# Four moves of work inside the blocks of a Mamba-style mixer with an MLP behind it: token copy, padded x, fold of squares, last half projection

## The reference, cut to what matters

```
x = x + mixer(layernorm(x))          # the part that the change touches
x = x + ffn(layernorm(x))            # silu(gate) * up, then down, inner width 1408

mixer:
  proj = x @ W_in * mup              # z (1024), xBC (1024+128+128), dt (64)
  xBC  = silu(causal conv of 4 taps) # gives x, B, C
  dt   = softplus(dt + bias);  dA = exp(-dt * exp(A_log))
  state = state * dA + (dt * x) outer B ;  y = state . C      # per token, 64 heads of 16
  g    = (y + D * x) * silu(z)
  g    = g * rsqrt(mean(g^2) + eps) * norm_w
  out  = g @ W_out
```

## Time and profile before

| what | value |
|---|---|
| median of the timed runs | 776.65 us |
| the profiled execution | 781.25 us |
| its span, first to last instruction | 779.5 us |
| mean granted TensorE clock | 0.987 |
| TensorE busy | 742.5 us, 95% of the span |
| VectorE, ScalarE, GpSimd busy | 66%, 63%, 38% |

### The profile page before, as it was taken

How to read it: one execution, slowest core, us unless ns; L and a number is a source line. 1 busy time by engine, 2 the same in 40 slices (tenths; PEclk the granted TensorE clock), 3 DMA queues, 4 the chain that set the end, 5 groups by cost and what they waited for, 6 DMA issues and landing times.

```text
span 779.5 us, 20312 instructions
## 1 busy us (share of the span) xinstructions
PE 742.5 (95%) x8486; PEld 611.1 (78%) x8486; DVE 517.5 (66%) x845; ACT 492.0 (63%) x933; POOL 294.5 (38%) x235
## 2 busy tenths in 40 slices
PE   4977999999999999999999999889999999999998
PEld 4855788788887887887878888668888888888887
DVE  6968976986887797797787698773633532632431
ACT  5989878978978977978878797633322321331330
POOL 3163275366456536627708628530011011001002
PEclk9988999999999999999999999999999999999999
DMA  9823244484475266355355367754113004002002
GB/s 304 228 62 109 45 102 112 96 235 130 82 215 163 79 146 209 101 148 187 109 160 185 108 182 241 227 168 155 62 49 114 0 28 132 3 3 94 11 1 84
DMA packets 42299, 94.97 MB, mean 122 GB/s; under 512 B 9888, under 2 KB 15776, under 8 KB 42016
## 3 DMA queue, kind: packets, MB, share of 16 engines
q1 hardware_dynamic: 42208, 93.67, 41.8%
HBM read 84.73 MB, written 17.57 MB: 131 GB/s over the span
## 4 chain that ended last, share of the span: by engine, by line
PE 72%; DVE 16%; ACT 6%; issue 3%; DMA 2%; SPq 1%; POOL 0%; DVEq 0%; ACTq 0%; POOLq 0%
PE ps_y L1678 10%; PE ps_proj L1665 9%; DVE cx L936 7%; PE ps_out L1665 6%; PE ps_x L1665 6%; PE ps_proj L1223 6%; PE ps_proj L1224 5%; PE ps_proj L1225 5%; PE ps_y L1295 4%; PE ps_x L1272 4%; PE ps_out L1319 3%; PE ps_x L1306 3%; PE ps_out L1321 3%; PE ps_out L1320 3%; DVE ring L991 2%
## 5 line engine op out<-in xcount | busy, mean ns | idle before, releaser
L530 POOL TENSOR_TENSOR ring<-tokd,ring 128x1024 f32<-128x1024 f32 x64 | 122.1, 1921 | 192.0 <-ACT tokd L710 129.5
L1223 PE MATMUL ps_proj<-xn_hi,win_x_hi 128*128 128x256 f32 x352 | 104.3, 296 | 1.5 <-DVE xn_lo L905 1.5
L1224 PE MATMUL ps_proj<-xn_lo,win_x_hi 128*128 128x256 f32 x352 | 101.0, 287 | 0.9 <-issue 0.9
L1225 PE MATMUL ps_proj<-xn_hi,win_x_lo 128*128 128x256 f32 x352 | 101.0, 287 | 0.0
L936 DVE SCALAR_TENSOR_TENSOR cx<-cin,consts,cx 128x256 f32<-128x256 f32 x240 | 96.4, 475 | 1.7 <-ACT cx L691 1.7
L1534 POOL TENSOR_TENSOR res<-res,hidden 128x512 f32<-128x512 f32 (+1 forms) x16 | 20.1, 1256 | 166.4 <-DVE hidden L1597 160.6
L1223 PEld LDWEIGHTS ps_proj<-xn_hi,win_x_hi 128*128 128x128 f32 x352 | 68.8, 196 | 14.4 <-issue 13.7
L991 DVE TENSOR_TENSOR ring<-ring,ps_tok 128x1024 f32<-128x1024 f32 x64 | 75.4, 1214 | 4.1 <-ACT ring L719 4.1
L1223 PE MATMUL ps_proj<-xn_hi,win_z_hi 128*128 128x256 f32 x256 | 74.0, 289 | 0.0
L1224 PE MATMUL ps_proj<-xn_lo,win_z_hi 128*128 128x256 f32 x256 | 72.3, 283 | 1.0 <-issue 1.0
L1225 PE MATMUL ps_proj<-xn_hi,win_z_lo 128*128 128x256 f32 x256 | 72.1, 282 | 0.0
(11 more groups left out here) (186 smaller groups left out, 1885.7 us busy)
## 6 DMA issues: line engine op xcount, KB each, us to landing
ring<-cum_dram SPq DMA_DIRECT2D x128, 256.0 KB, 4.7
xin<-x SPq DMA_DIRECT2D x8, 512.0 KB, 3.7
res<-x SPq DMA_DIRECT2D x32, 128.0 KB, 2.7
x_dram<-res SPq DMA_DIRECT2D x32, 128.0 KB, 3.0
res<-x_dram SPq DMA_DIRECT2D x16, 256.0 KB, 2.7
out<-res SPq DMA_DIRECT2D x15, 256.0 KB, 2.1
x_in_sb<-x_dram SPq DMA_DIRECT2D x3, 1024.0 KB, 5.6
gate_w_copy<-gate_w SPq DMA_DIRECT2D x4, 704.0 KB, 6.5
```

The source lines that it names most:

```text
L530: pool.tensor_tensor(ring[:, g, :, :], own, ring[:, g, :, :], ALU.subtract).then_inc(diffed, 1)
L1223: pe.matmul(out, hi[:, k, :], xn_hi[:, k, :], start=(k == 0), stop=False)
L1224: pe.matmul(out, hi[:, k, :], xn_lo[:, k, :], start=False, stop=False)
L1225: made = pe.matmul(out, lo[:, k, :], xn_hi[:, k, :], start=False, stop=(k == KT - 1))
```

## The change

Four moves, and one wait:

- ACT: in the first step of a block `keep_tok` stands ahead of `square` and `evacuate(i, 7)`.
- DVE: in the first step of blocks 2 to 7 `mask_cb` and `make_xpad` stand ahead of the two looks. `scale_carry` writes the buffer `rows`, which a look reads, and so waits for that look (VectorE itself; it has been issued before).
- POOL: `fold_squares` stands behind `make_xw` and `fade_state`, in all steps.
- PE, last block, second step: of the first half of `project_out(14)` two of the four tiles (six matmuls) stand between the second and the third group.

```diff
@@ POOL body
-                    if not opening:
-                        fold_squares(c - 1)
                     if not closing:
                         make_xw(i, j)
                     if not (opening or closing):
                         fade_state(i, j)
+                    if not opening:
+                        fold_squares(c - 1)
@@ ACT body, first step
                 clamp(c, 1)
+                keep_tok(c)
                 if not first:
                     square(c - 1)
                     evacuate(i, 7)
-                keep_tok(c)
@@ DVE scale_carry
                 dve.wait_ge(carry_added, c - 1)
+                if j == 0 and i - 1 in LOOKED:
+                    dve.wait_ge(hand.low_max_made, 3 * (i - 1) - 1)
@@ DVE body, first step
+                mask_cb(c)
+                make_xpad(i, 0)
                 if i - 1 in LOOKED:
                     low_max(i - 1, 0)
                     low_max(i - 1, 1)
-                mask_cb(c)
-                make_xpad(i, 0)
@@ PE body, second step of the last block
                 if last:
-                    project_out(c - 1, FIRST_HALF)
+                    project_out(c - 1, range(0, 2))
...
                 if last:
-                    for g in range(GROUPS):
-                        group(c, g)
+                    group(c, 0)
+                    group(c, 1)
+                    project_out(c - 1, range(2, 4))
+                    group(c, 2)
+                    group(c, 3)
                     sum_squares(c - 1)
```

## The result

The changed kernel takes 800.46 us (median of 5 runs, 800.4 to 809.81), the kernel before 777.47 in the same comparison (5 runs, 776.6 to 778.93). The ratio is 1.0318, with a 95% interval of 1.0261 to 1.0376. The forecast was 780.8 with a range up to 784.0: the sign was right, the size was not. The change costs some 23 to 25 us, not 4.

The account below looks back on a forecast made before the run. TensorE, busy 742.5 of 779.5 us, was taken as the bound, so only its idle time could be won. Second steps +4.5, first steps -0.6, split +0.2, fold 0 gave 776.65 + 4.1 = 780.8 us, 8-in-10 range 775.0 to 784.0.

Parts of the forecast that it names:

- Token copy and padded x ahead: First steps: the padded x comes earlier, TensorE's waits for it at first carries go; 1.3 to 2.8 us won.
- That just fits: Block 4, first step: make_x1 ends at 295.8, just when TensorE, its carry begun at 293.9, wants it.
- The looks later: Second steps, blocks 2 to 6: the later look at xin delays x load, store and ring loads; +4.5 us in sum.
- Rings 2.9 later. So 2.9 - 2.0 = +0.9.: Block 2, second step: ring loads start 2.9 us later, slack takes 2.0, leaving 0.9 us lost.
- rival (2): Each x1 store takes its 8.9 us again, block 4's perhaps 10.7: 782.8 to 784.6 us; chance 0.11.
- Rival (1): The x1 store lands 2.9 us after its issue, no second step suffers: 774.0 to 775.6 us; chance 0.22.
- The terms are waits, the same in both: Profiled and timed executions share the waits, so +4.1 applies to the timed 776.65, giving 780.8 us.
- The fold behind the fading: GpSimd's three moved sums are covered by TensorE's work with 6.0 us to spare: 0, at most 2.64 us.
- The split half projection: Last block: six matmuls change places, a short wait for group 1 is possible; +0.2 us, bounds -0.3 and +0.5.
- Rival (3): Last block, second half projection: TensorE's 3.6 us stall without a visible wait goes, at most 3.6 won: 777.2; chance 0.06.
- The sum: Over the whole kernel: +4.5 - 0.6 + 0.2 = +4.1 us, giving 780.8 us.

Follow-up runs that it names:

- copies late: The changed kernel with the two weight copies of blocks 2 to 6 issued behind the second step's ring loads: 782.88 us, ratio 1.006 to the kernel before.
- copies in the middle: The changed kernel with the two weight copies issued behind x1 store and residual load, ahead of the second step's ring loads: 802.73 us, ratio 1.0261.

## Why the prediction was wrong, step by step

**Token copy and padded x ahead.** Right in its places. First carries wait no more, and the half projection waits for `make_x1` (3.7 in four, longest 1.3; before there was one such wait, 1.8 in the last block). The gain forecast for this part, 1.3 to 2.8, is what the token copy brings by itself (2.8). The padded x ahead of the look at `rows` added nothing that can be told. "That just fits" was off: in blocks 4 and 5 TensorE waits 1.1 for `make_x1`, since its carry follows 0.1 behind the padded x, not 1.0.

**The looks later: the step that failed.** "Rings 2.9 later. So 2.9 - 2.0 = +0.9." The forecast for the second steps was +4.5; the five stretches from first to second carry grew by 17.9. The way of thinking (queue later, store's landing, ring loads, minus the slack) was the right one, but two of its terms came out short, and a third, what the copies cost the ring loads in transfer, was put at nothing. In block 2, counted from the first carry or the turn of x:
- The x load starts 4.25 later against the turn of x (170.23 - 166.10, and before 167.93 - 168.05), not 3.6 (in the other four blocks 3.65 to 4.35): the padded x began 0.6 behind the turn's end, because VectorE waited for ScalarE's copy (1.56 in the timeline above) and not for TensorE alone.
- The store reported 9.07 behind the load, not 8.5. I had argued that it need not take its 8.9 again; it took it in every block (9.07, 9.12, 10.54, 9.17, 9.06). That was rival (2), with 0.11 of the chance; its 782.8 to 784.6 was still far too low. By the Trainium skill, page "DMA: Bandwidth & Descriptors", section "Queues, rings and completion order", a semaphore's increment lands behind every earlier write of its engine, and here the measurements agree: 7.3 from issue to landing behind two copies, 2.95 with the copies late (block 2).
- The `diff` started 16.5 instead of 11.8 behind the carry, 4.7 later, of which 4.2 were the issue and 0.5 the transfer. 4.7 - 2.0 of slack = 2.7, and the second carry came 2.67 later (29.93 - 27.26). The slack of 2.0, at least, was right.

In block 5 the transfer cost more. The second ring load was in use only 8.3 after the loads began to be issued (376.08 to 384.38). A likely cause is that all eight went out within 6.2 us, where before they took 10.2, waiting in part for rings to be freed: that is read from the two timelines and was not tried by itself. The DMA rates fit it. Busy time by stretch in the changed kernel, the last three columns being TensorE's granted clock, DMA share and GB/s:

```profile
378.00:381.00 3.00, 3.00 (x92) 2.12 (x78) 1.69 (x4) 1.38 (x4) 0.00 (x0) 1.00 1.04 244
381.00:384.00 3.00, 2.75 (x30) 2.43 (x18) 2.96 (x3) 1.00 (x1) 1.90 (x1) 1.00 1.01 253
```

The forecast was 2.7 for blocks 2, 3 and 6 together, 0.4 for block 5 and 1.4 for block 4. The profile has 2.67 + 2.00 + 3.07 = 7.7, then 4.2 and 5.9. Block 4, which had no slack, was 4.5 short, and block 5 3.8. For block 4 the forecast had let the store land 2.2 sooner than before, after 8.5; it landed after 10.54, and even without copies it is the slowest of the five, so its old 10.7 was no sign of slack to be won. The first `diff` there is 5.5 later where the forecast had its rings 0.9 later. Rival (1), a store that lands on its own, is refuted by the queue's rows. The run with the copies in the middle gave the store what that rival wanted (in block 2 it landed 2.9 after its issue), and with the copies still ahead of the rings nothing was won. So the rival's reasoning was wrong too. In the changed kernel most of the delay does come by way of the store (4.2 of 4.7 in block 2), as the forecast had it; what was missing is that the copies are also paid for by every load behind them in the transfers.

**What idle time costs beyond itself.** Not in the forecast at all. "The terms are waits, the same in both" left out that behind its long waits TensorE's matmuls run slower for a while. Busy time by stretch in the changed kernel, same columns, behind the wait of 2.39 that ended at 199.88:

```profile
200.00:201.50 1.50, 1.50 (x8) 0.37 (x8) 1.50 (x2) 1.50 (x3) 1.50 (x1) 0.86 0.04 11
201.50:203.00 1.50, 1.50 (x7) 0.64 (x4) 0.64 (x2) 1.50 (x4) 0.76 (x2) 0.50 0.75 169
203.00:204.50 1.50, 1.50 (x9) 1.50 (x9) 1.50 (x2) 1.50 (x2) 1.50 (x1) 0.51 0.02 5
```

The granted clock, third from the end, is 0.50, which is the level of 1.2 GHz instead of 2.4, for some 3.4 us; from 204.5 it is 1.00 again. Behind block 1 there are five such stretches (after 199.88, 309.51, 395.64, 462.58 and the last block's waits) and in the kernel before there were two, at 393 and 516. Half the clock for 3.4 us costs some 1.7 us of busy time, an estimate from these rows. Three stretches more make 5.1, and TensorE's busy time rose by 5.0. Not every long wait has this price, and a short one can: in the kernel with the copies in the middle no stretch follows a wait of 2.53 (carry at 268.06), and the one at 393 follows an idle time of 1.04.

**The fold behind the fading.** Wrong. "TensorE's work covers it with 6.0 to spare ... 0." It looked only at who waits for the fold. The fold is covered, indeed nothing waits for it; but it is company for VectorE's small products in second steps, and those are on the path through the rings of the next block. +6.8 alone (in the changed kernel +6.3, give or take 5.6), over the bound of 2.64 that I had set. The Trainium skill, page "SBUF — State Buffer", section "Who interferes with whom", has the rule that I should have looked up: a VectorE instruction with two inputs in SBUF contends with a GpSimd instruction that reads SBUF. `dt_p<-dt_p,dt_e` has two such inputs and went from 299 to 394 ns on average, three of eight held until the sum beside them was over. `ring<-ring,ps_tok`, with one of its two inputs in PSUM, stayed at 1214 ns (1214 in the fold-alone run). Both agree with the rule.

**The split half projection.** Forecast +0.2, alone 1.0015 with an interval around 1: not contradicted. Rival (3) did not come: of the last block's stall of 3.6 at `ps_out` 2.4 are left in the changed kernel, but another of 1.9 now stands ahead of a group.

**The sum.** By the runs with a part taken back: looks +20.6, fold +6.3; by the runs of a part alone: token copy -2.8, split +1.2; together +25.3. By the runs of each part alone it would be 23.2 + 6.8 - 2.8 + 1.2 = 28.4. Measured: 3.18%, +24.7 with an interval of 4.5 to either side, which holds both. The forecast had +4.5, 0, -0.6 and +0.2. Three things were missing: the full price of the copies for the store and the rings, the fold beside the products, and the low clock behind long waits.

## What to carry to other kernels

Where an instruction on a quiet engine releases a queue, price the move by the last load behind it that someone needs, and by every large transfer in between, whether or not a wait ties them: here, with two weight copies of 704 KB between an x load and eight ring loads, starting the queue 4 us later in five blocks cost 20 us; with the copies behind the ring loads it cost nothing that could be told. Work that "nobody waits for" still has neighbours: look at what will run beside it, here GpSimd's sums beside VectorE's products. And four of the changed kernel's waits of 2.4 us or more each brought some 1.7 us of half clock with them, which belongs in the price of a wait.

## What the runs showed of the hardware

- A store of 2 x 128 KB behind two DRAM-to-DRAM copies of 704 KB reported 7.3 us after its issue (8.8 in block 4). With the copies late it was 2.95 (5.1 in block 4).
- A ring load right behind those copies reached its use 8.7 us after its issue, with the copies behind it 5.3, and 5.4 where it was issued 5.9 behind the copies.
- VectorE's products of 128x128 with both inputs in SBUF took 394 ns on average with GpSimd's sums beside part of them, against 299 without. One product beside each sum took 0.74, 0.77 and 0.50 us and ended 0.14 or 0.15 us behind it; the others took 0.29. Sums of 128x1024 with an input in PSUM took 1214 ns in both kernels.
- After idle times of 2.4 to 3.7 us TensorE was granted 0.50 of its clock for some 3.4 us. In the kernel with the copies in the middle one of 2.53 was not followed by it, and in the kernel before one of 1.04 was.
- The same block showed an unnamed stall of 3.66 in one kernel and a named wait of 3.3 in another, with equal step lengths. A stall's name is a weak guide to its cause; the distance between two landmarks of the program, here the carries, is a better one.
